# A two-layer graph attention kernel: the adjacency loads, issued from one queue, are issued from two

## The reference

```python
def layer0(h, W, a, adj):            # h = relu(layernorm(x))
    h = h @ W
    e = leaky_relu((h @ a_src)[:, None] + (h @ a_dst)[None, :], 0.2)
    valid = (adj > 0) & (h.sum(1) != 0)[None, :]
    att = where(valid, softmax(where(valid, e, NEG), 1), 0)
    att = where(att >= 1e-4, att, 0) * valid.sum(1)[:, None]
    return elu(h + att @ h)

def layer1(h, W, a, adj):
    Wh = h @ W
    e = leaky_relu((Wh @ a_src)[:, None] + (Wh @ a_dst)[None, :], 0.2)
    return softmax(where(adj > 0, e, NEG), 1) @ Wh

x = x + layer0(relu(layernorm(x)), W0, a0, adj)
x = x + layer1(relu(layernorm(x)), W1, a1, adj)
```

## Time and profile before

| | us |
|---|---|
| median of 3 runs (lowest to highest) | 2451.42 (2451.02 to 2457.12) |
| the profiled execution | 2455.78 |
| its span | 2454.0 |

### The profile page before, as it was taken

How to read it: one execution, slowest core, us unless ns; L and a number is a source line. 1 busy time by engine, 2 the same in 40 slices (tenths; PEclk the granted TensorE clock), 3 DMA queues, 4 the chain that set the end, 5 groups by cost and what they waited for, 6 DMA issues and landing times. The chain is left out here.

```text
span 2454.0 us, 38658 instructions
## 1 busy us (share of the span) xinstructions
PE 1957.3 (80%) x16852; PEld 1943.5 (79%) x16852; DVE 1611.6 (66%) x1861; ACT 822.6 (34%) x1212; POOL 4.5 (0%) x23
## 2 busy tenths in 40 slices
PE   1475659659677597686865946999999999999997
PEld 1365659659677597586865936999999999999997
DVE  4365548557575486565854856777777777777775
ACT  4755565655665656656556013000000000000000
POOL 0000000000000000000000000000000000000000
PEclk9687889889888898898887968999999999999999
DMA  9999999989989999899898223212221322222120
GB/s 192 229 264 277 278 288 250 256 258 286 315 226 271 280 273 275 244 303 297 232 253 262 87 80 150 101 70 89 84 87 69 98 86 77 87 87 87 69 70 11
DMA packets 164343, 447.54 MB, mean 182 GB/s; under 512 B 21696, under 2 KB 79424, under 8 KB 147520
## 3 DMA queue, kind: packets, MB, share of 16 engines
q1 hardware_dynamic: 164160, 444.94, 63.2%
HBM read 365.04 MB, written 79.82 MB: 181 GB/s over the span
## 5 line engine op out<-in xcount | busy, mean ns | idle before, releaser
L902 PE MATMUL psum<-h_all,arena 128*128 128x129 f32 x16384 | 1877.8, 278 | 349.0 <-DVE arena L895 349.0
L902 PEld LDWEIGHTS psum<-h_all,arena 128*128 128x128 f32 x16384 | 1871.6, 195 | 354.1 <-DVE arena L895 329.3
L895 DVE SCALAR_TENSOR_TENSOR arena<-arena,rho_col 128x1024 f32<-128x1024 f32 x1024 | 1294.4, 1279 | 328.8 <-PE psum L902 319.5
L207 ACT ACTIVATE arena<-arena,half_step 128x1024 uint8<-128x1024 int32 x512 | 720.0, 1434 | 532.3 <-DMA arena<-in_adj_dram 467.0
L220 DVE STREAM_TRANSPOSE arena<-arena 128x1024 f32<-128x1024 f32 x128 | 157.9, 1237 | 188.0 <-ACT arena L207 188.0
L1054 DVE SCALAR_TENSOR_TENSOR arena<-arena 128x1024 f32<-128x1024 f32 x8 | 9.8, 1226 | 206.0 <-ACT arena L983 206.0
L207 ACT ACTIVATION_READ_ACCUMULATOR arena<-arena,half_step 128x1 f32 x512 | 90.1, 176 | 0.0
L517 PE MATMUL psum<-arena 128*128 128x131 f32 x256 | 48.7, 351 | 39.2 <-ACT arena L486 39.2
L517 PEld LDWEIGHTS psum<-arena 128*128 128x128 f32 x256 | 43.4, 255 | 44.2 <-ACT arena L486 44.0
L509 PE MATMUL psum<-ident,arena 128*128 128x128 f32 x128 | 27.3, 353 | 54.8 <-DVE arena L391 54.8
L509 PEld LDWEIGHTS psum<-ident,arena 128*128 128x128 f32 x128 | 21.3, 187 | 56.1 <-DVE arena L391 55.3
(11 more groups left out here) (97 smaller groups left out, 123.5 us busy)
## 6 DMA issues: line engine op xcount, KB each, us to landing
arena<-in_adj_dram SPq DMA_DIRECT2D x1024, 256.0 KB, 7.4
edgesT<-arena SPq DMA_DIRECT2D x64, 1024.0 KB, 12.4
arena<-edgesT SPq DMA_DIRECT2D x64, 1024.0 KB, 4.8
arena<-r_mid SPq DMA_DIRECT2D x2, 3072.0 KB, 20.1
arena<-in_x_dram SPq DMA_DIRECT2D x16, 256.0 KB, 9.9
h_mid<-h_all SPq DMA_DIRECT2D x16, 256.0 KB, 3.2
arena<-h_mid SPq DMA_DIRECT2D x8, 512.0 KB, 14.5
arena<-in_x_dram SPq DMA_DIRECT2D x32, 128.0 KB, 8.2
```

The lines of the kernel that those rows point to most:

```text
L207: nc.scalar.activation(pack_bytes[h][:, k, a], adj_in[n % NA], ACT.Sigmoid, bias=half_step[:, 0:1], scale=STEEP, accum_out=cnt[g % 2][:, a ...
L895: return nc.vector.scalar_tensor_tensor(wT.rearrange("p (k n) -> p k n", k=BK), r_of(g), rho_col[:, j:j + 1], edge_bytes[:, (g * NSUB + j ...
L902: last = nc.tensor.matmul(acc_tile(g, k), wT[:, k * P:(k + 1) * P], h_all[:, j, :], start=(j == 0 and k % 2 == 0), stop=(j == T - 1), skip ...
```

## The change

`load_pair` gets an argument `half` and issues two of the four DMAs: `half` 0 those of partition groups 0 and 1, `half` 1 those of groups 2 and 3. Wherever SyncE called it, it now issues half 0. ScalarE issues half 1: three pairs ahead of its first mask, and then, after each odd piece that it has masked, the half pair that refills that buffer. It waits on the same value of `masked` as SyncE does, thus on its own mask that it has just issued. The masks wait for the same 64 on `adj_in_loaded` as before. Nothing else changes.

```diff
-        def load_pair(sp, n):
+        def load_pair(eng, n, half):
             g, c, h, k, a = piece(2 * n)
             if 2 * n >= NA:
-                sp.wait_ge(masked, 2 * n - NA + 2)
-            for b in (0, 2, 1, 3):
-                sp.dma_start(adj_pairs[n % (NA // 2)][b * BP:(b + 1) * BP],
+                eng.wait_ge(masked, 2 * n - NA + 2)
+            for b in (2 * half, 2 * half + 1):
+                eng.dma_start(adj_pairs[n % (NA // 2)][b * BP:(b + 1) * BP],
                              adj_pieces[g * G + 2 * k + h, a // 2, c, b]).then_inc(adj_in_loaded[n % (NA // 2)], 16)
...
                     if first:
+                        for m in range(NA // 2):
+                            load_pair(act, m, 1)
                         for m in range(NA):
                             mask_piece(act, m)
+                            if m % 2 == 1:
+                                load_pair(act, (m + NA) // 2, 1)
...
                 for chunk in range(1, NG * COLS):
                     for i in range(PIECES):
-                        mask_piece(act, chunk * PIECES + i)
+                        n = chunk * PIECES + i
+                        mask_piece(act, n)
+                        if n % 2 == 1 and n + NA < NG * COLS * PIECES:
+                            load_pair(act, (n + NA) // 2, 1)
                         if chunk % COLS == 1 and chunk > 1 and i == 26:
                             elu(chunk // COLS - 1)
```

More of the change, by code:

```diff
@@ L328, in _ @@
                             if i < NA // 2:
-                                load_pair(sp, i)
+                                load_pair(sp, i, 0)
                         else:
@@ L333, in _ @@
                         for m in range(NA // 2, NA):
-                            load_pair(sp, m)
+                            load_pair(sp, m, 0)
                         for q in range(Q):
@@ L339, in _ @@
                             if NA + q < (PIECES + NA) // 2:
-                                load_pair(sp, NA + q)
+                                load_pair(sp, NA + q, 0)
                     wait(sp, rows_ready, 2, 1)
@@ L959, in sync_rows @@
                         if ahead < NG * COLS * PIECES and ahead % 2 == 0:
-                            load_pair(sp, ahead // 2)
+                            load_pair(sp, ahead // 2, 0)
                         if i in (4, 7, 10, 13):
```

## The result

The change makes the kernel slower: 2477.91 us median (2477.39 to 2479.29, 3 runs) against 2451.42, a ratio of 1.0102 (95% interval 1.0079 to 1.0125). The forecast was 2394.

A forecast was written before the change was run, and what follows sets the result against it. Loads bind first, then ScalarE, VectorE, TensorE. Mixing and ScalarE's issues, -7 us over 8.3 groups, give -58 us: 2455.8 to 2398, or 2394 for the median; forecast range 2350 to 2435, outer range 2320 to 2505.

The forecast's parts named there:

- What bounds the kernel: Until about 1350 us, adjacency loads come first, then ScalarE, VectorE, TensorE; ScalarE waits 467 us for loads.
- the loads are mixed differently: Adjacency loads from two queues would reach 300 GB/s, winning 7 us per 160 us group, at most 25.
- over 280: Sign of being right: windows with loads alone move over 280 GB/s at a busy share near 1.
- under 200: Sign of being right: ScalarE's waits for loads fall from 467 us to under 200.
- TensorE's wait for VectorE: Sign of being right: this wait falls from 349 us by about 60.
- all engines in step: Before the change, each DMA engine takes one partition group's rows after the other's, in step; two queues might end that.
- ScalarE's cost: Issues and mask wait: 1.1 us per pair, 35 us per group; 7 uncovered if loads stay slow.
- rival B: Masks and exponential: loads stay slow, ScalarE becomes late, 5 us per group, 2492 us; chance 0.27.
- the wait for the exponential: Rival B's sign: VectorE's wait for ScalarE's exponential grows from 28.1 us in the group.
- Rival A: Adjacency loads get no faster and ScalarE's issues hide: 2451 us, or within 7; chance 0.13.
- The earlier issue: A pair's last DMA issued 0.9 us sooner from SyncE: 1 us per group, 8 us in all.

The follow-up runs named there:

- e2: Kernel before with a pair's four loads in the order 0, 1, 2, 3 instead of 0, 2, 1, 3, still on SyncE: 2532.6 us.
- e15: The change with whole pairs by turns, even from SyncE, odd from ScalarE, each in the order 0, 2, 1, 3: 2501.15 us.
- e10: Kernel before, one queue, each load split in two and alternating 0, 2, 0, 2, 1, 3, 1, 3: 2434.51 us.
- e16: Kernel before with the same eight split loads as e10, but ordered 0, 0, 2, 2, 1, 1, 3, 3: 2491.54 us.
- e7: Kernel before, all loads on SyncE; ScalarE waits for its own mask and runs three small activations per pair: 2454.19 us, ratio 1.0008.
- e8: The change with the first three pairs issued whole by SyncE between its x loads: 2474.26 us, ratio 1.0098.
- e5: The change with partition groups 2 and 3 issued by idle GpSimd instead of ScalarE: 2485.91 us, ratio 1.0153.
- e12: e8 with the stores of turned blocks also moved to GpSimd's queue: 2473.86 us, ratio 1.0074.
- e3: Kernel before, loads unchanged; ScalarE waits for its own mask and issues two tiny stores per pair: 2672.27 us, ratio 1.0917.
- e17: The change with each load split in two, SyncE 0, 0, 1, 1 and ScalarE 2, 2, 3, 3: 2532.16 us.
- e1: The change with SyncE issuing partition groups 0 and 2, ScalarE 1 and 3: 2520.31 us, ratio 1.0274.

## Why the prediction was wrong

**What bounds the kernel** held: loads, ScalarE, VectorE, TensorE, in this order. Wherever the waits for loads and the engine time rose, as in e2, the time rose with them (85 us and 80 us).

**The step that failed is "the loads are mixed differently", with its 7 us per group.** It took the second queue as a gain on top of today's order. But the diff removed an order as well as adding a queue: 0, 2, 1, 3, which alternates the partition halves, became 0, 1 and 2, 3. I had that line before me and priced only the queue. The order alone is worth 80 us (e2), and the two queues do no more than restore the engine time, 1551 against 1547 us. The stretches with loads alone stayed at 247 GB/s on the mean, where the forecast wanted over 280; ScalarE's waits for loads fell to 393 us, not under 200, and TensorE's wait for VectorE rose from 349 to 363 us. Keeping the old order would not have brought the gain either: e15 has it in both queues, and its engine time is 1552 us. So the 7 us per group had two faults, the order that was overlooked and a gain from the second queue itself, which no run shows.

The picture behind this step, all engines in step before the change, does not fit the trace either. Each of the 16 engines reports the end of its share of each load. Between 180 and 1300 us of the kernel before, when the last of a pair's 64 shares has landed, 14 of the next pair's 64 have landed already. So the engines are apart by about a whole load on the mean. No run shows that being in or out of step decides the rate; what they show is that the order of the groups does.

The rule in "DMA: Bandwidth & Descriptors" of the Trainium skill (rules for kernel authors), that spreading transfers over issuing engines and over partition halves gives no bandwidth, came out right for this change against the kernel before: the engine time agrees. Its other half, that such transfers simply serialize, says too little: the same packets differ by 101 us (before and e2) and 136 us (e10 and e16) with their order. The section on the DMA port swizzle in "SBUF — State Buffer" of the Trainium skill says that groups 0 and 1 share their ports and 2 and 3 theirs, and the sign of both pairs of runs agrees with it. That the ports are the cause is not shown. The groups also differ in the matrix columns that they read, and no run put the same columns into other partitions.

**ScalarE's cost** was sized well, 1.05 us per pair for 1.1 (0.85 us for the issues, the rest for the accumulator read and the semaphore). How much of it comes through is open. The forecast let 7 us per group through, and rival B 5. With one queue of loads the buffers carried 0.75 us per pair at no loss (e7). In the change 91 masks waited for ScalarE's own issues, and the whole loss is 26 us, 3.2 per group.

**Rival B** said slower, 2492, and is the nearest of the rivals. Its premise held: the loads stayed as slow, and ScalarE is late more often (below). Its sign that the wait for the exponential grows did not: 27.8 us in the group for 28.1, and 204 us for 206 in all. VectorE's wait for masks grew, from 188 to 205 us. Rival A, whose engine time came out, expected the issues to hide.

**The earlier issue**, 8 us kept out of the sum, shows nowhere.

**The start** was not in the forecast: six loads that ScalarE issues at 6.3 us go beside SyncE's x loads and first half pairs, and the first mask is 4.9 us later. The total hardly hangs on it (e8).

**Where the change's 22 to 26 us go** can be read from the landings in the traces, between 180 and 1300 us. "Landed" is the time from the moment at which a pair's buffer came free to its last load, "lying" from there to the start of its first mask; both are means. "Close" counts the pairs that landed less than 2.8 us, the time of two masks, behind the pair before.

| | landed, us | lying, us | pairs lying over 0.6 us | close |
|---|---|---|---|---|
| before | 11.4 | 0.8 | 30 of 220 | 6 |
| the change | 11.0 | 1.6 | 103 of 218 | 29 |
| e7, 0.75 us more on ScalarE | 11.2 | 1.0 | 41 of 222 | 4 |
| e5, two queues, nothing more on ScalarE | 11.7 | 0.9 | 49 of 217 | 26 |
| e15, whole pairs by turns | 10.7 | 2.0 | 112 of 215 | 26 |

In the change a pair does not land later; it lies longer, until ScalarE comes. With two queues the pairs land unevenly, whoever issues the second half (e5): the seven such versions with loads of 256 KB have 20 to 29 close pairs, the versions with one queue of loads at most 6. ScalarE's issues alone, on pairs that land evenly, cost little (e7). The change has both, and two pairs that land close behind each other meet a ScalarE that needs 3.80 us for each. This fits all five rows, but that the two act together is argued: e5, which takes the issues off ScalarE, has GpSimd's slower ones in their place, and its loads land later.

**What stays open** is how the loss divides between uneven landing and ScalarE's issues, of which 0.3 us per pair was never tried. The first pairs do not explain it, to within the intervals (e8), and the stores at most in part (e12).

## What to carry to other kernels

When a diff changes the queue, compare the order of the transfers too, group by group: here the order in one queue was worth 80 us, three times what the whole diff cost. Before moving issues to spread them, compute the engine time (share of the DMA engines times the span), which tells cheaper transfers from better overlap. Where transfers of 32 partitions bound a kernel, try to alternate partitions below and above 64 as finely as the issues allow, from a queue that has room for them; it paid in both comparisons here. Try one queue first for loads that one consumer waits for: each of the nine versions with two queues of loads was slower than the kernel before.

## What the runs showed of the hardware that was not expected

- 506 tiny stores from a second queue, of 32 x 8 bytes each and 0.7% of the engines' time, made the other queue's packets take 1763 us per engine instead of 1551, and the kernel 220 us slower (e3).
- The same 180544 packets took 1468 or 1604 us per engine, by the order of eight issues (e10, e16).
- Two issues behind a pair of masks kept ScalarE idle for 0.93 us; in their place 0.71 us of small activations cost the kernel nothing (e7). Four issues made ScalarE the bound, 435.7 us of "issue" waits (e17).
- Loads of 32 partitions alone, on all 16 engines at a busy share near 1, moved 226 to 275 GB/s on the mean, by how the same bytes were ordered, split and queued (e1 and e10, stretches of 10 us between 180 and 1300 us).
- Pairs that come through two queues land unevenly: 29 of 218 land less than 2.8 us behind the one before, for 6 of 220 from one queue, though the mean time to land falls from 11.4 to 11.0 us (the change).
- The kernel before spread over 0.25% in its first 3 runs, but over 1.0% in 18 runs and 1.4% in 10 runs beside the experiments, so a gain of 4 us as in e8 could not be told.
